# TensorE's programs of the two long stages written as hardware loops, edge weights one block a pair, three mask buffers instead of four

## What is computed

```python
# layer 0, sums over neighbours (x here is layer-normed)
neigh = jax.ops.segment_sum(node_feats[src], dst, num_segments=n)
h = (1.0 + eps) * node_feats + neigh          # then two dense layers, batch norm
...                                           # experts of layer 0 (top 2 of 16)
# layer 1, messages weighted by an MLP of each edge
h = jax.nn.silu(edge_scalars @ fc_w1 * ...) * SILU_NORM
w = h @ fc_w2 * ...                           # 4 x 64 weights an edge
mid0 = w_a * xg0 * ea0                        # xg = y[edge_src], ea = edge_attr
mid1 = w_b * jnp.einsum('euc,ec->eu', xg1, ea1) * INV_SQRT3
mid2 = (w_c * xg0)[:, :, None] * ea1[:, None, :]
mid3 = (w_d * ea0)[:, :, None] * xg1
agg = jax.ops.segment_sum(mids, edge_dst, num_segments=n)
...                                           # dense layers, then one of 8 experts a node
```

## Time and profile before

| | us |
|---|---|
| median of 3 timed runs | 1999.44 (1993.48 to 2000.63) |
| span of the profiled execution | 2413.3 |
| sums over neighbours and edge weights | 0 to 722 |
| dense layers, batch norm, experts of layer 0 | 722 to 1248 |
| messages | 1248 to 2057 |
| dense layers, routing, last experts | 2057 to 2413 |

### The profile page before, as it was taken

The page is one execution under the profiler, slowest core; times in us unless marked ns, Lnnn a source line. Parts: engine busy times, 40 slices in busy tenths (PEclk is TensorE's granted clock), DMA queues, the critical chain, the costliest instruction groups (busy, mean ns, idle before and its releaser), DMA issues. The chain is left out here.

```text
span 2413.3 us, 38460 instructions
## 1 busy us (share of the span) xinstructions
PE 1891.3 (78%) x9911; PEld 1517.9 (63%) x9911; DVE 1125.8 (47%) x2791; ACT 1021.4 (42%) x3052; POOL 1104.5 (46%) x1499
## 2 busy tenths in 40 slices
PE   1368787877799858999455877787778789899699
PEld 1245454554466657999335766676767679777588
DVE  3532222222242374544664666565656669431322
ACT  2513343343353532333264555454545557454222
POOL 5547667666700004555375665565655550000243
PEclk7679999889999858999777888887888889999799
DMA  5636556565734026666544554555554553255553
GB/s 150 202 90 198 190 187 198 185 193 187 210 140 138 11 64 201 212 212 215 135 149 147 150 159 140 151 155 145 147 153 144 150 148 107 69 164 177 155 180 129
DMA packets 229197, 376.43 MB, mean 156 GB/s; under 512 B 66081, under 2 KB 114308, under 8 KB 228998
## 3 DMA queue, kind: packets, MB, share of 16 engines
q1 hardware_dynamic: 174820, 222.13, 31.0%
q0 software_dynamic: 52224, 150.15, 20.2%
q10 hardware_dynamic: 1954, 1.79, 0.2%
HBM read 275.38 MB, written 99.57 MB: 155 GB/s over the span
## 5 line engine op out<-in xcount | busy, mean ns | idle before, releaser
L1940 POOL DMA_INDIRECT msg_got<-y_dram,block_src x416 | 412.4, 991 | 293.5 <-DVE msg_prod L2012 139.7
L439 POOL DMA_INDIRECT ffn_w<-xn_dram,block_src x384 | 364.6, 949 | 219.2 <-issue 81.7
L1961 ACT ACTIVATE msg_scaled<-msg_plain,msg_w 128x125 f32<-128x125 f32 x1044 | 314.0, 386 | 280.1 <-DVE msg_plain L1993 234.6
L554 PE MATMUL sum_ps_bank<-ffn_w,sum_onehot 128*125 x928 | 270.5, 419 | 115.6 <-DVE sum_onehot L893 84.3
L554 PEld LDWEIGHTS sum_ps_bank<-ffn_w,sum_onehot 128*125 128x125 f32 x928 | 184.0, 206 | 264.6 <-issue 246.6
L881 DVE TENSOR_TENSOR agg<-sum_ps_bank,agg 125x256 f32 x232 | 98.4, 424 | 432.4 <-PE sum_ps_bank L554 216.5
L541 PE MATMUL sum_ps_bank<-sum_fc,sum_space 128*128 128x512 f32 x416 | 231.9, 644 | 68.9 <-ACT sum_space L639 48.3
L650 ACT ACTIVATE sum_space<-sum_ps_bank,sum_rec 128x128 f32<-128x128 f32 x416 | 131.0, 369 | 330.4 <-PE sum_ps_bank L541 159.5
L1982 PE MATMUL msg_ps_z<-msg_prod,msg_scaled 128*125 128x128 f32 x1416 | 207.5, 293 | 53.7 <-issue 53.0
L1982 PEld LDWEIGHTS msg_ps_z<-msg_prod,msg_scaled 128*125 128x125 f32 x1416 | 198.6, 206 | 72.4 <-issue 64.1
L2022 DVE TENSOR_TENSOR agg<-msg_ps_z,agg 125x512 f32 x232 | 159.4, 687 | 23.9 <-issue 5.2
(11 more groups left out here) (343 smaller groups left out, 3397.9 us busy)
## 6 DMA issues: line engine op xcount, KB each, us to landing
edge_w<-sum_space SPq DMA_DIRECT2D x52, 1040.0 KB
msg_w<-edge_w SPq DMA_DIRECT2D x174, 260.0 KB
ffn_run_w<-in_L_ffn_w SPq DMA_DIRECT2D x64, 512.0 KB
x_sb<-edge_w SPq DMA_DIRECT2D x58, 260.0 KB
ffn_rows<-agg SPq DMA_DIRECT2D x25, 448.0 KB
ffn_w<-in_L_ffn_w SPq DMA_DIRECT2D x16, 512.0 KB, 8.7
wd<-in_L_ffn_Wd SPq DMA_DIRECT2D x8, 1024.0 KB, 8.6
msg_got<-y_dram,block_src POOLq DMA_INDIRECT x416
```

The source lines that it names most:

```text
L439: pool.indirect_dma_start(got[:, (b + 1) % RING, u, :], None, k.x if b < RAW else k.xn_dram, bass.IndirectOffsetOnAxis(ap=k.block_src[:, b ...
L554: last = pe.matmul(ps_sum[n % ZB][0:P, :], onehot[n % OB][:, u, :], got[:, ds(need % RING, 1), u, :].rearrange("p o d -> p (o d)"), start= ...
L1940: pool.indirect_dma_start(got[:, (b + 1) % RING, u, :, :].rearrange("p k v -> p (k v)"), None, k.y_dram, bass.IndirectOffsetOnAxis(ap=k.bl ...
L1961: last = act.activation(scaled[s % MB][:, x, c, :], plain[s % MB][:, c, :], ACT.Copy, scale=w[s % RS][:, c, D + x:D + x + 1])
```

## The change

Three edits; DVE's, ACT's, POOL's and SP's programs keep their instructions.

1. In `sum_neighbours`, `edges_due` now asks for two edge blocks a pair in pairs 30 to 41 (EARLY = 24), none in pairs 42 and 43, then one a pair in pairs 44 to 227. So 24 pairs are alike but for offsets, and pairs 44 to 211 become a loop on PE of 7 turns of 24 pairs. Within the loop the waits compare with a register instead of a constant.
2. In `sum_messages`, PE's steps 0 to 2 and the last two stand straight, steps 3 to 113 become a loop of 37 turns of three steps (`pe.Fori(1, 38)`).
3. MB goes from 4 to 3, so that masks, products and PSUM banks come round in three steps. The lent buffer moves from index 1 to 2.

```diff
-    EDGES_FROM, EDGES_TO = 30, 226
+    EDGES_FROM, LOOP_FROM, LOOP_PAIRS, EARLY = 30, 44, 24, 24
+    LOOPS = (NB - EARLY) // LOOP_PAIRS
...
     def edges_due(n):
-        return min(NB, max(0, (n + 1 - EDGES_FROM) * NB // (EDGES_TO - EDGES_FROM)))
+        if n < LOOP_FROM:
+            return min(EARLY, max(0, 2 * (n + 1 - EDGES_FROM)))
+        return min(NB, EARLY + n + 1 - LOOP_FROM)
...
-            for n in range(NPAIR):
-
-                need = pe.value_load(k.pair_need[0:1, n:n + 1], min_val=1, max_val=NB)
+            def sums(n, trip=0):
+                at = n + trip * LOOP_PAIRS
+                need = pe.value_load(k.pair_need[0:1, n:n + 1] if isinstance(at, int) else k.pair_need[0:1, ds(at, 1)], min_val=1, max_val=NB)
                 pe.wait_ge(blocks_in, need)
...
-                pe.wait_ge(masked, n + 1)
+                pe.wait_ge(masked, at + 1)
...
+            for n in range(LOOP_FROM):
+                sums(n)
+                for e in range(edges_due(n - 1), edges_due(n)):
+                    edge_block(e)
+            with pe.Fori(0, LOOPS) as trip:
+                for j in range(LOOP_PAIRS):
+                    sums(LOOP_FROM + j, trip)
+                    edge_block(EARLY + j, trip, last_trip=False)
+            for n in range(LOOP_FROM + LOOPS * LOOP_PAIRS, NPAIR):
+                sums(n)
+                for e in range(edges_due(n - 1), edges_due(n)):
+                    edge_block(e)
...
-    RS, MB, ZB, XB = 4, 4, 6, 3
+    RS, MB, ZB, XB = 4, 3, 6, 3
...
-            for s in range(NST):
-                pe.wait_ge(scaled_made, s + 1)
-                pe.wait_ge(made, s + 1)
-                if s >= ZB // 2:
-                    pe.wait_ge(added, 1 + 2 * (s - ZB // 2 + 1))
+            def step(turn, j, first=False):
+                pe.wait_ge(scaled_made, turn * MB + j + 1)
+                pe.wait_ge(made, turn * MB + j + 1)
+                if not first:
+                    pe.wait_ge(added, turn * 2 * MB + 2 * j - 2 * MB + 3)
...
+            for j in range(MB):
+                step(0, j, first=True)
+            with pe.Fori(1, NST // MB) as turn:
+                for j in range(MB):
+                    step(turn, j)
+            for j in range(NST % MB):
+                step(NST // MB, j)
```

More of the change, by code:

```diff
@@ L518, in _, with turn, first_layer @@
             pe.transpose(ps_tot[:, 0:VEC_ROWS], rows[:, :], k.ident[0:VEC_ROWS, 0:VEC_ROWS]).then_inc(cols_ready, 1)
-            def turn(g):
-                pe.wait_ge(rec_in[g % RB], 16 * (g // RB + 1))
+            def turn(g, trip=0):
+                pe.wait_ge(rec_in[g % RB], 16 * (g // RB + 1) + trip * 16 * LOOP_PAIRS // (QB * RB))
                 if g >= 1:
-                    pe.wait_ge(kept, g)
+                    pe.wait_ge(kept, g + trip * LOOP_PAIRS // QB)
                 pe.transpose(ps_t[:, :], rec[g % RB][:, :, :, :].rearrange("p b u w -> p (b u w)"), k.ident[:, :])\
                   .then_inc(turned, 1)
-            def first_layer(g):
-                pe.wait_ge(kept, g + 1)
+            def first_layer(g, trip=0):
+                pe.wait_ge(kept, g + 1 + trip * LOOP_PAIRS // QB)
                 if g >= 1:
-                    pe.wait_ge(hid_made, g)
+                    pe.wait_ge(hid_made, g + trip * LOOP_PAIRS // QB)
                 for b in range(QB):
@@ L557, in _, with edge_block @@
                 last.then_inc(summed, 1)
[L558 to L572, removed]
+            def edge_block(e, trip=0, last_trip=True):
+                g, b = e // QB, e % QB
+                if e == 0:
+                    pe.wait_ge(fc_in, 16 * 10)
+                    pe.wait_ge(fc2_made, 8)
+                    pe.wait_ge(cols_made, 2)
+                    turn(0)
+                    turn(1)
+                    first_layer(0)
+                if b == 0 and (g + 2 < NW or not last_trip):
+                    turn(g + 2, trip)
+                if b == 2 and (g + 1 < NW or not last_trip):
+                    first_layer(g + 1, trip)
+                second_layer(g, b, trip)
+            pe.wait_ge(tables_made, 1)
+            for n in range(LOOP_FROM):
[10 more added lines that the diff above has]
+                    edge_block(e)
         @block.scalar
@@ L1871, in sum_messages @@
     assert LAG + 2 < AHEAD
-    RS, MB, ZB, XB = 4, 4, 6, 3
+    RS, MB, ZB, XB = 4, 3, 6, 3
+    assert MB == XB == ZB // 2
     LAST = NPAIR // 2 - 3
-    assert LAST % RS == LAST % MB == 1 and LAST % XB == 2
+    assert LAST % RS == 1 and LAST % MB == LAST % XB == 2
     CH = 2 * KC
@@ L1889, in sum_messages @@
              for b in range(RS)]
[L1890 removed]
+        plain = [borrow(CH * P).rearrange("p (c w) -> p c w", c=CH) if b == 2 else ph.sb(f"plain{b}", [128, CH, P])
                  for b in range(MB)]
[L1892 removed]
+        scaled = [borrow(3 * CH * P).rearrange("p (x c w) -> p x c w", x=3, c=CH) if b == 2 else ph.sb(f"scaled{b}", [128, 3, CH, P])
                   for b in range(MB)]
@@ L1967, in _ @@
             pe.matmul(ps_lanes[:, :], k.onesf[0:1, :], k.iota[0:1, 0:P], start=True, stop=True).then_inc(lanes_made, 1)
-            for s in range(NST):
-                pe.wait_ge(scaled_made, s + 1)
-                pe.wait_ge(made, s + 1)
-                if s >= ZB // 2:
-                    pe.wait_ge(added, 1 + 2 * (s - ZB // 2 + 1))
-                mask, by, p = plain[s % MB], scaled[s % MB], prod[s % XB]
+            def step(turn, j, first=False):
[3 more added lines that the diff above has]
+                    pe.wait_ge(added, turn * 2 * MB + 2 * j - 2 * MB + 3)
                 for h in range(2):
-                    z = ps_z[(2 * s + h) % ZB]
+                    z = ps_z[2 * j + h]
                     for u in range(KC):
                         c = KC * h + u
-                        pe.matmul(z[0:P, 0:4, :], mask[:, c, :], p[:, c, 0:4, :], start=(u == 0), stop=False, skip_group_check=True)
+                        pe.matmul(z[0:P, 0:4, :], plain[j][:, c, :], prod[j][:, c, 0:4, :], start=(u == 0), stop=False, skip_group_check=True)
                     for x in range(3):
@@ L1981, in _ @@
                             c = KC * h + u
-                            last = pe.matmul(z[0:P, 4:6 + x:1 + x, :], by[:, x, c, :], p[:, c, 4 + x:8:3 - x, :],
+                            last = pe.matmul(z[0:P, 4:6 + x:1 + x, :], scaled[j][:, x, c, :], prod[j][:, c, 4 + x:8:3 - x, :],
                                              start=False, stop=(x == 2 and u == KC - 1), skip_group_check=True)
                 last.then_inc(summed, 1)
+            for j in range(MB):
[5 more added lines that the diff above has]
+                step(NST // MB, j)
         @block.vector
```

10 lines of the change are left out of this document (5 added, 5 removed).

## The result

| | us |
|---|---|
| before, median of 11 runs | 1998.69 (1993.48 to 2000.63) |
| changed, median of 11 runs | 2001.06 (1997.36 to 2005.92) |
| ratio | 1.0027, 95% interval 1.0015 to 1.0039 |

The change costs 0.27%, 5.4 us (3 to 8): slower as forecast, but less than half of the 12 us. Within the 0.5% that the prediction named, it is no change. The two medians by themselves differ by 2.4 us and the means by 4.1; the ratio and its interval are the recorded estimate from all runs of both, and they are what this text goes by.

A forecast was written before the change was run, and what follows sets the result against it. It took DVE to bound the messages, PE 5% behind, and POOL's gathers or PE, which are close, the sums. 10 for edge blocks, 2 + 1 for masks, less 1, on 1999.4 gave 2011 us; range 1962 to 2040.

The forecast's parts named there:

- the 0.5% that the prediction named: Whole kernel: about 10 us is what a measurement can tell from no change; its three runs span 7 us.
- The reading of the profile: Sums and messages: timed runs hold hardly any of the profile's PE waits; messages run at about 4.57 us a step.
- The 392 us of waits: Profiled excess: 267 us of PE waits in the messages plus 125 of PE's lateness in the sums.
- The rival that part of them is real: PE's late instructions also occur in timed runs and a loop ends them: 39 us faster, about 1960; chance 0.25.
- Edge blocks drawn forward: Sums, pairs 30 to 41: doubled blocks slow PE and hold POOL, losing 10 us, bounds 0 and 10.
- the ring was already full when the edge blocks began: Sums: POOL, already waiting on PE, is let go about 12 pairs, 10.8 blocks, where it wants 14.7.
- the 7.16 us of the earlier trace: Sums: POOL's wait on PE at 165.17 in the profile before, taken as showing the ring full.
- Three mask buffers: Messages: 0.22 us left for two hand-overs; waits 0 to 5 us, taken as 2, plus 1 at the start.
- Loops: PE in sums and messages: loops remove waits for its own instructions, of which timed runs have none: 0.
- Turns: PE's loops, 44 branches: covered by matmuls still running, so 0; uncovered, 10 us.
- The rival that turns fetch: PE's loops: each turn fetches its body anew with PE standing, 50 us on top of 12, about 2060; chance 0.05.
- less 1: Sums: 1 us taken off the total for the two light pairs, 42 and 43, without edge blocks.

The follow-up runs named there:

- two_turns: Kernel before with three mask buffers and PE's messages steps as a loop of two turns of 54 steps; ratio 1.0027 (1.0013 to 1.0041).
- messages_only: Kernel before with only the messages' edits, three mask buffers and the three-step loop, sums as before; ratio 1.0004 (0.9991 to 1.0018).

## Why the prediction was half right

**The reading of the profile held.** The 392 us of waits were not in the timed runs: two further profiles of straight programs (1998.1, 1995.3) have none of them. The rival that part of them is real fell. But the profiler as such did not slow the kernel, as the text ahead of the prediction had it: it was one execution. What disturbed it stays open.

**Edge blocks drawn forward: mechanism right, 10 us were 2.8.** A doubled pair takes PE 3.1 us on average, as worked out, and POOL is held through the ring. The step that failed is "the ring was already full when the edge blocks began". It rested on the 7.16 us of the earlier trace rows, and these belong to the disturbed execution: there the sum of pair 31, which lets that block go, ended 17.2 us after the sum of pair 30, with the first edge blocks between the two; undisturbed it ended 5.2 us after it, 6.0 in the changed kernel. The ring was not full. By the rule `b − 7`, block 38 may be gathered when pair 30 is summed. In the changed kernel that was at 103.63 + 2.83 = 106.46, and POOL came to this block 8.0 us later:

```profile
103.63 2.83 PE L557 MATMUL sum_ps_bank<-ffn_w,sum_onehot 128*125 x9
114.47 0.95 POOL L444 DMA_INDIRECT ffn_w<-xn_dram,block_src  x1 [0.17 <-issue]
```

The next 12 pairs took PE 40.4 us, until 146.88, which let block 50 go at 147.16. POOL wants 12 × 2.51 = 30.1 us for 12 blocks. Of the 10.3 us by which PE was slower, the lead of 8.0 swallowed 7.7, and the rest, 2.6, reached POOL: these are the five waits above, which begin only at block 46. There was a second slip in the same sum: it lets 10.8 blocks go in 12 pairs, but by `b − 7` each summed pair lets one block go, so that 37 us of PE against 12 blocks of POOL are 6.9 us and not 10.

**Three mask buffers: mechanism right, PE's step mis-sized; 3 us were 3.6 with the loop and 7.0 straight.** I took PE's step as 4.35 and the two hand-overs as 0.16 to 0.30. 4.35 is PE's pace from step to step when it never waits. With three buffers it waits for DVE's additions in nearly each step and starts with an empty pipe. Its first weight load after the wait in the changed kernel, shown above, starts at 1403.18. That step's last group is

```profile
1406.33 1.47 PE L1999 MATMUL msg_ps_z<-x_sb 128*125 128x128 f32 x12
```

From the weight load to the end of this group, 1406.33 + 1.47 = 1407.80, are 4.62 us, and DVE's next mask starts at 1407.84. A mask waits for the PE step that began when DVE had ended the step before last; so two steps take DVE's 4.57 and PE's side together, and 9.37 means that PE's side is 4.80, or 4.86 straight. The hand-overs in it, 4.80 − 4.62 = 0.18, lie inside what I had. What failed is the 4.35: from a standing start PE's step is 4.62.

That the net is near the 3 is luck. Summed over the last 105 steps, the masks of the changed kernel come 13.5 us later than at 4.575 a step, far over the 0 to 5 that I gave to these waits. But with four buffers they come 8 to 11 us later as well (five profiles), in another form, which the prediction did not have: some 20 steps take 0.2 to 1 us more, because the gathered rows are late (in about three quarters of them the product that stands follows POOL's word on its rows by the same 0.30 us). These waits are gone when DVE is held by PE instead. Net, by stages: 555.8 us (mean of three profiles) against 552.2 (of five), and 559.2 straight (of three).

**Loops: 0 in the sums, right; in the messages 3 us back, which I had at 0.** They come from the waits, not from turning: two of three are cleared on register operations ahead of the matmul, and with them PE starts 0.06 us sooner after DVE (`two_turns`).

**Turns: covered, right.** The rival that turns fetch falls for these bodies, and `two_turns` shows where it would hold. There two instruction packets of PE moved in the 10 us around the branch (DMA, 1354 to 1364):

```profile
q8 instruction: 2, 0.03, 1.4%
```

while from the second turn on the loops of 24 pairs, 3 steps and 12 steps have no row of this queue at all. The Trainium skill, "Runtime: NRT & Kernel Launch", "Instruction fetch mechanics", says that a taken branch to a target outside the current window of two pages stalls until it is fetched. The trace agrees for the body of 54 steps, at 4.1 us for its one turn. It doesn't for the bodies of 24 pairs and 12 steps: they have some 600 and 800 instructions in the trace, more than two packets of the prediction's 256, and still turned in 0.2 us with no packet.

**The sum.** 2.8 for the sums and 3.6 for the messages make 6.4, against 5.4 (3 to 8) measured, where the prediction had 10 and 3, less 1. What the forecast had too much lies in the edge blocks' term alone, the one with the ring taken as full: it was 7 us too large, and the masks' term 0.6 too small. `messages_only` measured 0.8 us (−1.8 to 3.6), its 3.6 at the edge of the interval, though its profile shows them; why the timed runs show less stays open.

## What to carry to other kernels

Before any stall of a profile is explained, hold its span against the timed runs; where they differed by a fifth, here, the order of events in it (which ring was full, who was ahead) was as untrustworthy as the totals. When a buffer is taken away, the pace to compare is not the back-to-back step of the engine behind it but its step from a cold start, with its first weight load and the hand-overs: here 4.8 instead of 4.35, where DVE's step is 4.57. And the loops on TensorE were cheap as long as no turn had to fetch its body, but what had to be bent to make the turns alike (blocks drawn forward, a buffer fewer) was the price; with a longer turn and an earlier start no loss was left that the runs could tell (0.9998, to 0.14%).

## What the hardware showed

A branch back took 0.2 us with bodies of 3 and 12 steps and of 24 pairs, with no instruction packet, and 4.1 us with one of 54 steps, with two packets beside it. Two waits on a register operation ahead of a matmul, in place of the matmul's own, let PE start 0.05 instead of 0.12 us after DVE's additions. A step of PE took 4.62 us from a standing start where its pace from step to step was 4.35. A gather of 128 rows took POOL 0.95 us and 0.30 to the next, and a memset of 0.14 us between them cost nothing.
